# Group attention: the exponentials are scaled by their inverse sums on GpSimd before they are transposed

## What is computed

```python
q = hidden_state @ Wq + bq                  # 32 heads of 16 features
k = encoder_hidden_state @ Wk + bk          # 8 heads, each for 4 query heads
v = encoder_hidden_state @ Wv + bv
scores = jnp.einsum('bkgld,bksd->bkgls', q, k) * scale
scores = scores + encoder_attention_mask[:, :, None, :, :]
attn = jax.nn.softmax(scores, axis=-1)
out = jnp.einsum('bkgls,bksd->bkgld', attn, v)
...
x = out @ Wo + bo + hidden_state
return (x - mu) * jax.lax.rsqrt(var + EPS) * gamma + beta
```

## Time and profile before

| | us |
|---|---|
| median of three runs | 3284.5 (3279.46 to 3285.76) |
| the profiled execution, its own time | 3284.93 |
| its span, first to last instruction | 3283.2 |
| PE busy in the span | 3063.1 (93%) |
| DVE busy | 2073.4 (63%) |
| ACT busy | 1241.9 (38%) |
| POOL busy | 942.3 (29%) |
| stretch 1117 to 1493, the group phase: PE, DVE, ACT, POOL busy | 326.50, 290.66, 239.21, 86.73 of 376 |

### The profile page before, as it was taken

The page is one execution under the profiler, slowest core; times in us unless marked ns, Lnnn a source line. Parts: engine busy times, 40 slices in busy tenths (PEclk is TensorE's granted clock), DMA queues, the critical chain, the costliest instruction groups (busy, mean ns, idle before and its releaser), DMA issues. The chain is left out here.

```text
span 3283.2 us, 58784 instructions
## 1 busy us (share of the span) xinstructions
PE 3063.1 (93%) x21440; PEld 2224.2 (68%) x21440; DVE 2073.4 (63%) x3074; ACT 1241.9 (38%) x4419; POOL 942.3 (29%) x645
## 2 busy tenths in 40 slices
PE   8999899989999889985899999997799999999999
PEld 5666566668999856654676777674455555499998
DVE  5555455564544478884899999998254464574543
ACT  3444334432322366762343443442243333332322
POOL 3333233332000012222666666666000000030000
PEclk9999899999999999997999999998899999999999
DMA  4110141110000241111111111110230111011010
GB/s 177 42 42 28 58 157 55 48 39 23 16 26 16 84 155 47 51 38 65 46 41 40 52 52 37 41 49 30 68 140 28 31 34 37 23 49 39 19 38 13
DMA packets 104317, 170.31 MB, mean 52 GB/s; under 512 B 16512, under 2 KB 54016, under 8 KB 100736
## 3 DMA queue, kind: packets, MB, share of 16 engines
q1 hardware_dynamic: 99296, 124.58, 12.0%
q10 hardware_dynamic: 4896, 44.04, 3.3%
HBM read 135.03 MB, written 33.55 MB: 51 GB/s over the span
## 5 line engine op out<-in xcount | busy, mean ns | idle before, releaser
L2754 POOL TENSOR_TENSOR rec_S<-rec_S,rec_r_t 128x1024 f32<-128x1024 f32 x128 | 305.9, 2390 | 256.3 <-DVE rec_S L3081 255.0
L3081 DVE TENSOR_TENSOR_SCAN rec_S<-rec_decay,rec_S 128x1024 f32<-128x1024 f32 x128 | 303.5, 2372 | 8.2 <-DVE rec_S L3066 2.1
L1550 ACT ACTIVATE group_scores<-group_scores,group_negmax 128x128 f32<-128x128 f32 x512 | 197.6, 391 | 30.6 <-DVE group_negmax L1645 30.6
L635 ACT ACTIVATE latent_scores<-latent_scores,region_a 128x256 f32<-128x256 f32 x256 | 126.4, 497 | 71.7 <-DVE region_a L822 71.7
L635 ACT ACTIVATE self_scores<-self_scores,self_negmax 128x128 f32<-128x128 f32 x256 | 98.7, 390 | 77.0 <-DVE self_negmax L822 77.0
L635 ACT ACTIVATE cross_scores<-cross_scores,cross_negmax 128x128 f32<-128x128 f32 x256 | 98.8, 390 | 76.4 <-DVE cross_negmax L822 76.4
L2155 ACT ACTIVATE mlp_h_t<-mlp_h_t,vectors 128x128 f32<-128x128 f32 x256 | 81.3, 390 | 114.6 <-DVE mlp_h_t L2250 92.2
L2155 ACT ACTIVATE pmlp_h_t<-pmlp_h_t,vectors 128x128 f32<-128x128 f32 x256 | 81.3, 390 | 114.1 <-DVE pmlp_h_t L2250 91.7
L3386 PE MATMUL rec_rec_out<-rec_S,head_sum 128*32 128x256 f32 x1024 | 84.9, 404 | 41.9 <-POOL rec_S L2754 40.8
L3066 DVE TENSOR_TENSOR rec_S<-rec_vb,rec_k 128x1016 f32<-128x1016 f32 x96 | 115.2, 1200 | 0.0
L1007 PE MATMUL latent_pjA<-latent_src_t,F_query_key 128*128 128x512 f32 x240 | 114.4, 600 | 0.0
(11 more groups left out here) (489 smaller groups left out, 7915.9 us busy)
## 6 DMA issues: line engine op xcount, KB each, us to landing
rec_vb<-v_by_head SPq DMA_DIRECT2D x32, 512.0 KB, 4.3
region_a<-in_C_w ACTq DMA_DIRECT2D x2, 4096.0 KB, 19.9
region_a<-in_G_w ACTq DMA_DIRECT2D x2, 4096.0 KB, 19.2
self_xres<-in_x SPq DMA_DIRECT2D x16, 256.0 KB, 2.7
cross_ctx_t<-in_ctx_t SPq DMA_DIRECT2D x16, 256.0 KB, 3.3
cross_xres<-rows_A SPq DMA_DIRECT2D x16, 256.0 KB, 2.6
mlp_x<-rows_B SPq DMA_DIRECT2D x16, 256.0 KB, 2.7
group_ctx_t<-in_ctx_t SPq DMA_DIRECT2D x16, 256.0 KB, 3.2
```

Source lines behind the costliest of these rows:

```text
L635: nc.scalar.activation(S[:, u, at, :], S[:, u, at, :], ACT.Exp, bias=negmax[:, u, at.start // KB:at.start // KB + 1], accum_out=rowsum[:, ...
L1550: nc.scalar.activation(S[:, u, at, :], S[:, u, at, :], ACT.Exp, bias=negmax[:, u, at:at + 1], accum_out=rowsum[:, u // UPS, sum_column(u, ...
L2754: nc.gpsimd.tensor_tensor(S[u % 4][:, :, :], S[u % 4][:, :, :], bcast(r_t[:, s.k, UNITS[u][0], :], [128, JH, T], 1), ALU.mult)\
L3081: nc.vector.tensor_tensor_scan(St[:, :, :].rearrange(flat), decay[m][:, :, :].rearrange(flat), St[:, :, :].rearrange(flat), 0.0, ALU.mult, ...
```

## The change

The inverse no longer meets the output but the exponentials. DVE inverts the sums of one unit at a time (`invert`, those of unit 0 in two parts). POOL multiplies the exponentials with them in place, a quarter of four heads (128x512) an instruction (`scale_probs`), and PE transposes a quarter only when it has been scaled (`probs_scaled` takes the place of `exp_done`). The transposes of the inverse sums, their two items in the ring of banks P and Q, their copies and the spread on POOL go. The multiply with the output becomes a copy (`gather`). The sums lie in a buffer for each unit, in the order of the heads.

```diff
@@ banks @@
-                            ("t", 1, 0), ("t", 1, 1), ("t", 1, 2), ("t", 1, 3), ("ri", 0),
+                            ("t", 1, 0), ("t", 1, 1), ("t", 1, 2), ("t", 1, 3),
...
-                            ("t", 3, 0), ("t", 3, 1), ("x", 0), ("x", 1), ("t", 3, 2), ("t", 3, 3), ("ri", 1)]
+                            ("t", 3, 0), ("t", 3, 1), ("x", 0), ("x", 1), ("t", 3, 2), ("t", 3, 3)]
@@ GpSimd @@
-            def spread_inverse(it, k):
-                pool.wait_ge(rinv_done, it * 2 + k + 1)
...
+            def scale_probs(it, u, groups=range(4)):
+
+                for r in groups:
+                    pool.wait_ge(rinv_done, (it * U + u) * 2 + r // 2 + 1)
+                    heads = S[:, u, :, :].rearrange("p (i r) t -> p i r t", r=4)[:, :, r, :]
+                    nc.gpsimd.tensor_tensor(heads, heads, bcast(rowsum[:, u, 4 * r:4 * r + 4], [128, 4, T], 2),
+                                            ALU.mult).then_inc(probs_scaled, 1)
 
             def body(it):
+                scale_probs(it, 1)
                 if not is_first(it):
                     scale_output(it - 1, 0)
-                spread_inverse(it, 0)
                 residual_bias(it, 0)
+                scale_probs(it, 2)
+                scale_probs(it, 3)
                 if not is_first(it):
                     norm_scale(it - 1, 1)
-                spread_inverse(it, 1)
+                if has_later(it, 1):
+                    scale_probs(it + 1, 0, [0, 1])
                 if not is_first(it):
                     scale_output(it - 1, 1)
                 residual_bias(it, 1)
+                if has_later(it, 1):
+                    scale_probs(it + 1, 0, [2, 3])
                 norm_scale(it, 0)
 
+            scale_probs(0, 0)
             run_ahead(pool, body)
@@ ScalarE, exponentials @@
-                if part == 0 and u % UPS == 0:
-                    wait_count(act, rinv_spread, it * 2 + u // UPS - 1)
+                wait_count(act, probs_scaled, ((it - 1) * U + u) * 4 + 2 * part + 2)
@@ VectorE @@
-            def invert_sums(it, k):
...
+            def invert(it, u, begin=0, end=PARTS):
+
+                dve.wait_ge(exp_done, (it * U + u) * HU + end * HP)
+                heads = slice(begin * HP, end * HP)
+                nc.vector.reciprocal(rowsum[:, u, heads], rowsum[:, u, heads]).then_inc(rinv_done, end - begin)
+
+            def gather(it, k):
                 dve.wait_ge(pj.full_sem(("pv", k)), pj.uses_with(it, ("pv", k)))
-                nc.vector.tensor_tensor(o_t[:, k, :, :].rearrange("p c t -> p (c t)"), pj.bank(("pv", k))[:, :],
-                                        ri[:, :], ALU.mult).then_inc(pj.free_sem(("pv", k)), 1)
+                nc.vector.tensor_copy(o_t[:, k, :, :].rearrange("p c t -> p (c t)"), pj.bank(("pv", k))[:, :])\
+                    .then_inc(pj.free_sem(("pv", k)), 1)
@@ TensorE @@
-                pe.wait_ge(exp_done, it * U * HU + u * HU + 4 * (r + 1))
+                pe.wait_ge(probs_scaled, (it * U + u) * 4 + r + 1)
...
-            def spread_sums(it, k):
...
-                spread_sums(it, 0)
                 weigh_values(it, 1, 3)
...
                 weigh_values(it, 3, 2)
-                spread_sums(it, 1)
                 weigh_values(it, 3, 3)
```

More of the change, by code:

```diff
@@ L1330, in slots @@
         return [4 * r + b for r in range(4)]
-    def sum_column(u, j):
-        return (2 * (u % 2) + j // 8) * 8 + 2 * (j % 4) + j // 4 % 2
     def is_last(it, k):
@@ L1362, in group_phase @@
         negmax = sb("negmax", [128, U, HU])
-        rowsum = sb("rowsum", [128, SL, NH])
-        rinv = rowsum
+        rowsum = sb("rowsum", [128, U, HU])
         PT = sb("probs_t", [128, 4, 4, 128])
-        ri = sb("ri", [128, D])
-        rinv_by_feature = sb("rinv_by_feature", [128, D])
         o_t = sb("o_t", [128, SL, C, T])
@@ L1400, in group_phase @@
         rinv_done = sem("rinv_done")
-        rinv_spread = sem("rinv_spread")
+        probs_scaled = sem("probs_scaled")
         normed = sem("normed")
@@ L1550, in exponentials @@
                     nc.scalar.activation(S[:, u, at, :], S[:, u, at, :], ACT.Exp, bias=negmax[:, u, at:at + 1],
-                                         accum_out=rowsum[:, u // UPS, sum_column(u, j):sum_column(u, j) + 1])\
+                                         accum_out=rowsum[:, u, j:j + 1])\
                         .then_inc(exp_done, 1)
@@ L1681, in body @@
                 else:
-                    normalise(it - 1, 1)
+                    gather(it - 1, 1)
                 values(it, 0)
@@ L1688, in body @@
                 copy_probs(it, 0, 2)
+                invert(it, 1)
                 scale_and_mask(it, 2)
@@ L1695, in body @@
                 copy_probs(it, 1, 0)
-                invert_sums(it, 0)
                 copy_probs(it, 1, 1)
@@ L1700, in body @@
                 row_max(it, 3, 0)
+                invert(it, 2)
                 row_max(it, 3, 1)
-                copy_inverse(it, 0)
                 copy_probs(it, 2, 0)
@@ L1706, in body @@
                     key_blocks(it + 1, 0)
-                normalise(it, 0)
+                gather(it, 0)
                 copy_probs(it, 2, 1)
@@ L1711, in body @@
                 copy_probs(it, 2, 2)
+                invert(it, 3)
                 if later:
@@ L1722, in body @@
                 copy_probs(it, 3, 0)
-                invert_sums(it, 1)
+                if later:
+                    invert(it + 1, 0, 0, 1)
                 copy_probs(it, 3, 1)
@@ L1732, in body @@
                     row_max(it + 1, 1, 1)
+                    invert(it + 1, 0, 1, 2)
                 output(it, 0)
-                copy_inverse(it, 1)
             key_blocks(0, 0)
@@ L1741, in _ @@
                 row_max(0, u, 1)
+            invert(0, 0)
             run_ahead(dve, body)
-            normalise(NIT - 1, 1)
+            gather(NIT - 1, 1)
             output_stats(NIT - 1, 0)
@@ L1848, in weigh_values @@
                     last.then_inc(pj.full_sem(("pv", k)), 1)
-            def spread_sums(it, k):
-                begin(it, ("ri", k))
-                pe.wait_ge(rinv_spread, it * 2 + k + 1)
-                for c in range(C):
-                    last = nc.tensor.transpose(pj.bank(("ri", k))[:, c * 128:c * 128 + 128],
-                                               rinv_by_feature[:, c * 128:c * 128 + 128], ident)
-                last.then_inc(pj.full_sem(("ri", k)), 1)
             def body(it):
```

6 lines of the change are left out of this document (removed).

## The result

The changed kernel takes 3291.45 us (median of 8 runs, 3287.56 to 3293.95), the kernel before 3283.96 us in the same job (8 runs, 3279.24 to 3286.09). The ratio is 1.0024, with a 95% interval of 1.0014 to 1.0034: 7.5 us slower, where the forecast said 1.3 us. The profiled execution has a span of 3289.2 us against 3283.2 us.

A forecast was written before the change was run, and what follows sets the result against it. PE was taken as nearly the bound (39.88 of 42.69 us per iteration). The sum was 3284.9 + 6.3 (fill) - 4.1 (transposes) - 0.4 (bank) - 0.5 (drain) = 3286.2 us, stated as 3286, range 3279 to 3293.

The forecast's parts named there:

- the likeliest case: The forecast itself, 3286 us, chance 0.48, with its own range of 3283 to 3290.
- the port: Rival: DVE lets two POOL multiplies pass before normalising sequence 1's output, +5.6 us, 3292; chance 0.15. The forecast charged nothing.
- a fill or a multiply above its bound: Fill over 7.5 us or multiply over 1.28 us; given a tenth within the 0.22 chance of above 3291 us.
- The fill: Iteration 0: PE's first transposes wait for sixteen exponentials, a reciprocal and a multiply; 6.3 us lost, bounds 5.5 and 7.5.
- Nothing absorbs it: Claim that iteration 0 makes up none of the fill's delay; the opposing rival said 3280 to 3282, chance 0.13.
- The removed transposes: PE, iterations 0 to 6: only the first inverse-sum group counts, 7 x 0.59 = 4.1 us gained; rival counting both, chance 0.09.
- the 0.05 us of the bank: Iterations 0 to 6: the values product finds its bank free about 0.05 us earlier, 7 x 0.05 = 0.4 us gained.
- The multiply: Sixteen new 128x512 POOL multiplies per iteration, taken as 1.2 us each, bounded by 1.05 and 1.28; POOL busy 27.9 us.
- Unit 2 is the tightest, charged nothing: Steady loop: unit 2's first scaled quarter arrives 0.05 to 0.25 us before PE wants it, so no cost.
- The rival of 1.6 us multiplies: Unit 2's first quarter 0.35 us late in seven iterations, fill 0.4 us longer: 3289; chance 0.15.
- Units 0, 1 and 3 have more of PE's other work between their exponentials and their transposes: Claim that the new wait for exponentials, reciprocal and multiply costs these units nothing; read from one steady iteration.
- The drain: Iteration 7: t(2,0) starts 2 us later, mostly hidden in a bank wait; 0.7 remain against 0.59 and 0.6: -0.5 us.

The follow-up runs named there:

- The wait alone: Kernel before, with each unit's transposes waiting for all 16 exponentials and no multiply in front: 3291.46 against 3283.87 us, ratio 1.0028.
- the longer multiply: Changed kernel with an extra 128x256 GpSimd instruction in front of each multiply: 3297.49 us, ratio 1.0039.
- the weight move: 13 next-phase weight transfers issued by the sync engine, not ScalarE: kernel before 3278.63 us (second job 3276.66), changed kernel 3278.11 us.
- the later reciprocals: Changed kernel where, in iteration 1 alone, VectorE makes unit 1's reciprocals after scaling and reducing unit 2's scores: 3286.60 us, ratio 1.0010.

## Why the prediction was right and wrong

The measured 3291.45 us lies in the stated range of 3279 to 3293, but the sum said 1.3 us slower and 7.5 were measured. It is above the 3283 to 3290 of the likeliest case. What the forecast named for times above 3291 us (the port, a fill or a multiply above its bound) didn't happen. That the range held is luck: its upper end was there for the port, and a cause that the forecast didn't have filled it.

- *The fill*: right. 6.3 us were forecast; the table shows 5.75 at the first product and 6.5 at the end of iteration 0. "Nothing absorbs it" holds. The wait alone makes 4.8 of it. But the sum takes 0.64 us off in iteration 0, which leaves 5.7 us by its end, and 6.48 were measured: 1.4 us come on top behind the last product ahead of unit 3, most of them with the waits in front of t(3,0) and t(3,1).
- *The removed transposes*: right. Only the first group counts; 0.65 us per iteration with the 0.05 us of the bank, the forecast's 0.59 + 0.05. It holds for iterations 2 to 6 (3.4 us) and in iteration 0 up to unit 3 (5.75 to 5.07 us), where it is lost again; the sum counted seven.
- *The multiply*: 1.04 us, not 1.2, so POOL is busy for 25.02 us per iteration, not 28. The lower bound was the right row: an operand repeated along the keys costs as little as two of them, and two full ones 1.28 us. The Trainium skill (GPSIMD Engine Reference, section 3.1) gives about 2.6 cycles per element for two inputs; an estimate from it, at the 1.2 GHz that the section reckons with, is 1.11 us for 512 elements. No run here shows that value: the rows lie on either side of it.
- *Unit 2 is the tightest, charged nothing*: right. Its room was about 0.15 us, within the 0.05 to 0.25 us, and the longer multiply went beyond it into each iteration.
- *The port*: right. Normalisations take 0.93 and 0.54 us. The rival of 1.6 us multiplies fell with the measured 1.04 us.
- **The step that failed**: "Units 0, 1 and 3 have more of PE's other work between their exponentials and their transposes", with "In iterations 0 to 6 that is 7 x 0.59". Both were read from one steady iteration and carried over to all. In iteration 1 unit 1's exponentials stand behind 12.1 us of weight issue, and there is no other work left on PE: it had run out and already waited 1.27 and 4.42 us. The change makes one wait of 7.45 us out of these, and puts DVE's wait for sixteen exponentials ahead of unit 2's scores: +4.9 us. Shown by the weight move, which takes 12.9 us off iteration 1 here and 7.3 in the kernel before, so that the loss is gone, and by the later reciprocals (-2.5 us). The same step fails in a small way in iteration 0, where unit 3 has too little other work ahead of it and PE waits 0.51 and 0.37 us.
- *The drain*: -0.5 us was forecast, +2.4 and -0.1 us were measured in two profiles. The 2 us delay of t(2,0) came as said, and PE waited 2.30 and 2.05 us; the forecast hid most of that in a wait for a bank. The granted clock of 0.53 and 0.60 behind it was not in the sum either.

With 6.5 + 4.9 - 3.4 and a drain between -0.1 and +2.4 the phase loses 7.9 to 10.4 us at its last product, and one wait less at its end returns 0.3. Against the median's 7.5 us up to 2.6 us stay open; the traces show differences of that size in PE's clock outside the changed code, and I didn't separate them further.

## What to carry to other kernels

A steady iteration prices what is repeated; before multiplying by the number of iterations, look at the first ones for work that stands in a queue only once, such as a next phase's weight issue. When a change turns "wait for the first quarter" into "wait for all, then two more steps", its price is paid wherever the producer is late, and by all that stands behind the wait on each engine. Put the wait behind work that is ready.

## What was unexpected of the hardware

- Issuing 13 weight transfers takes 12.1 us on ScalarE's queue, where the engine then stood idle for 10.83 us, and 11.6 us on the sync engine's.
- A GpSimd multiply of 128x512 with one repeated operand takes 1.04 us, that with two full ones 1.28 us.
- PE's clock varies between executions of one program. The kernel before with the weight move lost 2.9 us in iteration 0 in one of its two profiles (a granted clock of 0.66 there, below) and nothing in the other (1.00 in its stretch from 1145 to 1155). A single profile can't size an effect of 3 us by its span; the markers within it narrow down where the time goes, but they too hold stretches of low clock.

```profile
1145.00:1155.00 10.00, 9.17 (x55) 0.66 1.01 390
```
